# Latent attention with a ternary feed-forward layer on one core: queries and keys stored as scaled 16-bit high and low parts

## The chip, the core and the metric

The kernel runs on one core of a Trainium2 chip. A core has five engines that run their own instruction streams and meet at semaphores: TensorE (PE; its weight loads are listed as PEld), VectorE (DVE), ScalarE (ACT), GpSimd (POOL) and SyncE (SP), which here only issues transfers. Operands lie in SBUF (128 partitions), matmul results in PSUM. The metric is the device time of one launch in microseconds (us), lower is better.

## What is computed

Two sequences (B = 2) of S = 1024 tokens with D = 256 features go through latent attention with H = 16 heads, a layer norm, a feed-forward layer with ternary weights and a second layer norm:

```python
c_kv = x @ w_dkv;  c_q = x @ w_dq                      # ranks 64 and 192
k_r = rope((x @ w_kr)); q_r = rope(c_q @ w_qr)         # 64 rotary features a head
k_n = c_kv @ w_uk;      q_n = c_q @ w_uq               # 128 plain features a head
scores = einsum('bqhd,bkhd->bhqk', [q_r,q_n], [k_r,k_n]) / sqrt(192)
out = einsum('bhqk,bkhd->bqhd', softmax(scores), c_kv @ w_uv) @ w_o
x = layernorm(x + out)
h1 = x @ t(w1).T; h3 = x @ t(w3).T                     # t(w): ternary weights, HID = 682
y = layernorm(x + (silu(h1) * h3) @ t(w2).T)
```

The attention weights are drawn eight times as large as usual, so the scores are large and their products are made to more than 16 bits: every large operand is kept as a high part and a low part, and a product is made of three terms (high by high, high by low, low by high).

## The kernel before

**Shape of the work.** The products w_uq by w_uk and w_uv by w_o of a head are formed once at the start, so that a head's keys are the 64 latent rows of c_kv under the 64 rotary rows: one key matrix K of 128 rows by 1024 columns serves all heads, and a head's query is a matrix of 128 rows by 1024 columns. The launch has a setup and then a loop over the two batches b, each of which has three stages: the projections (55 to 106 us of the span in the first batch, 518 to 568 in the second), the attention (to 438 and 900) and the output with the feed-forward layer.

**The projections.** `query_terms(g, j, ks)` makes one tile of the queries, ten matmuls of 512 columns (five terms, two column halves), for group g = 0 to 3 of four heads. The tiles j = 0 and 1 are the even and odd rotary rows of four heads, written to the PSUM banks Sa and Sb; the tiles j = 2 and 3 hold the latent rows of two heads each, in Ta/Tb and Oa/Ob. Each pair of banks is used again by the next group, so PE waits until it has been read. DVE multiplies Sa and Sb with the tables of cosines and sines into `qmul` (four products a group, L769, counted by `rope_mul`); POOL adds and subtracts these into `turned` (L361, `rope_sum`), and SP moves `turned` by eight transfers into QO, the queries in fp32. ACT copies the latent rows from Ta/Tb and Oa/Ob into QO (`lat_out`). `turn_values()` transposes the scaled latents of the keys into Oa (eight small matmuls, L1037); ACT and DVE read V_hi and V_lo from it. Before this DVE makes the rotary keys (L724 to L729) into Kf, their largest value and the scale of the values (L741 to L754), and K_lo from K_hi (L757).

**The attention.** A pair p of heads has 16 tiles n of 128 queries, in two half pairs of eight. For a tile: `scores` (six matmuls of 512 columns, L1054) fills Sa or Sb in turn, for the tile two ahead; `maximum` on DVE (a reduction L774, and one operation on a column L777); `exponent` on ACT (L552); `part_high` on ACT (L451) and `low_probs` on POOL (L385) make the 16-bit parts `P_parts` of columns 256 to 1023, which SP transposes by a transfer (L310, `part_in`); columns 0 to 255 are transposed on PE (L1065) and split by ACT (`PT_hi`, L451) and DVE (`PT_lo`, L784). `values` (L1083) sums over the keys for the half pair before, twelve matmuls after every second tile. There are `DEEP` = 4 buffers of probabilities and parts: `part_high` of tile n waits until the transposing transfer of tile n - 4 has landed, and `exponent` of tile n until `low_probs` of tile n - 4 is done. Where a half pair begins, DVE also normalises the sums of the half pair before last (L797, L799) and inverts the sums of the exponentials (L791), ahead of the next `maximum`.

The queries of a pair are split for the scores while the pair before runs: POOL copies four pieces of QO of 512 columns into Q_hi (fp32r, L353) and subtracts them into Q_lo (L347); for the first pair of a batch ACT makes the high parts.

**The output.** `project_out` (L1183) multiplies O_parts with Wvo_hi and Wvo_lo. Wvo_lo was saved to memory at the start, and its place is taken by K_hi and K_lo; ACT issues the transfer back (L605) after the last scores. SP issues xr (the input rows for the residual) and TT (the ternary weights) after the last transposing transfer, and then, in the first batch, Wq_hi and Wq_lo, since their places were overlaid with buffers of the attention.

Everything is written by hand: the order on an engine is the order of the code, and each engine takes its instructions strictly in that order. All transfers that SP issues go through one hardware queue.

## Time and profile before

| | us |
|---|---|
| median of three runs | 986.65 (984.76 to 988.56) |
| time of the profiled execution | 981.67 |
| its span, first to last instruction | 980.0 |
| PE busy | 918.8 (94%) |
| ACT / POOL / DVE busy | 680.4 / 672.0 / 633.7 |
| one pair of heads, 252.26 to 293.99 | 41.73 |

The profile tells for each engine when an instruction began and how long it was busy, and what ended the idle time before it. Busy PE time is a model: matmuls overlap, so the distance between the starts of two matmuls tells more than their length. The mean granted clock of TensorE was 0.989 of full speed. The chain of waits, followed back from the end of the program, runs 56% over PE, 10% over ACT, 9% over DVE, 5% over POOL and 2% over transfers.

### The profile page before, as it was taken

The numbers are of one execution on the slowest core, as the hardware profiler recorded it, in microseconds if no ns is written. First come the engines' busy times: TensorE is split into PE (matmuls) and PEld (weight loads), VectorE is DVE, ScalarE is ACT, GpSimd is POOL, SyncE is SP. The second block draws the span as 40 slices with busy tenths as digits, with TensorE's granted clock in tenths as the row PEclk, the third lists the DMA queues.
The fourth block names the chain that finished last, engine by engine and source line by source line (L and its number), as shares of the span: only waits on it lengthen the run. The fifth ranks groups of instructions, "written<-read, shape, count | busy, mean of one in ns | idle before, by whom it ended". The sixth has DMA issues, their size and how long they took to land.

```text
span 980.0 us, 17588 instructions
## 1 busy us (share of the span) xinstructions
PE 918.8 (94%) x5110; PEld 637.5 (65%) x5110; DVE 633.7 (65%) x1008; ACT 680.4 (69%) x1140; POOL 672.0 (69%) x503
## 2 busy tenths in 40 slices
PE   6799899999999999979989989999999999998985
PEld 3558666666666666658776866666666666666874
DVE  1665677777776677744457667777777777773455
ACT  3735988888878888851334598888878888875132
POOL 0007788988888989760341778889898988875034
PEclk9999999999999999999999999999999999999998
DMA  9834798888787887999000579888787787889201
GB/s 254 260 156 113 141 167 156 147 152 152 150 155 144 152 152 145 160 177 346 16 25 23 129 140 165 149 156 158 144 159 148 147 152 150 151 155 194 118 1 43
DMA packets 419814, 142.24 MB, mean 145 GB/s; under 512 B 405596, under 2 KB 413616, under 8 KB 418736
## 3 DMA queue, kind: packets, MB, share of 16 engines
q1 hardware_dynamic: 418160, 131.11, 67.8%
q10 hardware_dynamic: 1024, 8.39, 2.2%
q0 software_dynamic: 576, 2.10, 0.6%
q8 instruction: 25, 0.41, 0.2%
q14 instruction: 29, 0.24, 0.1%
HBM read 24.38 MB, written 8.13 MB: 33 GB/s over the span
## 4 chain that ended last, share of the span: by engine, by line
PE 56%; issue 15%; ACT 10%; DVE 9%; POOL 5%; DMA 2%; ACTq 1%; DVEq 1%; POOLq 0%
PE Sa L1054 14%; PE Sb L1054 12%; PE Oa L1083 9%; DVE nmax L774 5%; ACT P_parts L451 3%; POOL P_parts L385 3%; ACT probs_a L552 3%; PE Sb L1107 2%; PE Tb L1065 2%; PE Sa L1107 2%; DMA Wvo_lo<-wvo_low 2%; POOL g_lo L427 2%; PE Ta L1065 1%; PE Ob L1093 1%; ACT PT_hi L451 1%
## 5 line engine op out<-in xcount | busy, mean ns | idle before, releaser
L385 POOL TENSOR_TENSOR P_parts<-probs_a,P_parts 128x768 f16<-128x768 f32 x128 | 211.5, 1652 | 43.3 <-ACT P_parts L451 42.1
L385 POOL TENSOR_TENSOR P_parts<-probs_b,P_parts 128x768 f16<-128x768 f32 x128 | 211.6, 1655 | 36.8 <-ACT P_parts L451 36.6
L774 DVE TENSOR_REDUCE nmax<-Sb 128x1 f32<-128x1024 f32 x128 | 156.8, 1225 | 58.2 <-PE Sb L1054 58.2
L774 DVE TENSOR_REDUCE nmax<-Sa 128x1 f32<-128x1024 f32 x128 | 154.8, 1210 | 37.8 <-PE Sa L1054 37.7
L1083 PE MATMUL Oa<-PT_dma,V_hi 128*64 128x512 f16 x768 | 132.3, 385 | 0.0
L552 ACT ACTIVATE probs_b<-Sa,nmax 128x1024 f32<-128x1024 f32 x64 | 71.3, 1114 | 68.4 <-DVE nmax L777 68.2
L361 POOL TENSOR_TENSOR turned<-qmul 128x1024 f32<-128x1024 f32 x16 | 38.1, 2402 | 104.0 <-DVE qmul L769 104.0
L451 ACT ACTIVATE P_parts<-probs_a 128x768 f16<-128x768 f32 x128 | 107.8, 842 | 0.4 <-DMA PT_dma<-P_parts 0.4
L451 ACT ACTIVATE P_parts<-probs_b 128x768 f16<-128x768 f32 x128 | 107.3, 840 | 0.0
L1054 PE MATMUL Sa<-K_hi,Q_hi 128*128 128x512 f32 x256 | 93.1, 445 | 10.0 <-ACT probs_b L552 9.3
L1054 PE MATMUL Sb<-K_hi,Q_hi 128*128 128x512 f32 x256 | 93.5, 446 | 7.2 <-ACT probs_a L552 4.5
L552 ACT ACTIVATE probs_a<-Sa,nmax 128x1024 f32<-128x1024 f32 x64 | 71.4, 1115 | 30.9 <-DVE nmax L777 30.8
L347 POOL TENSOR_TENSOR Q_lo<-QO,Q_hi 128x512 fp32r<-128x512 f32 x64 | 82.2, 1288 | 10.5 <-POOL Q_hi L353 10.5
L1054 PE MATMUL Sa<-K_lo,Q_hi 128*128 128x512 f32 x256 | 80.3, 395 | 0.0
L1054 PE MATMUL Sb<-K_lo,Q_hi 128*128 128x512 f32 x256 | 80.2, 394 | 0.0
L1054 PE MATMUL Sb<-K_hi,Q_lo 128*128 128x512 f32 x256 | 80.0, 394 | 0.0
L1054 PE MATMUL Sa<-K_hi,Q_lo 128*128 128x512 f32 x256 | 79.6, 392 | 0.0
L784 DVE TENSOR_TENSOR PT_lo<-Ta,PT_hi 128x512 f16<-128x512 f32 x64 | 44.3, 692 | 54.6 <-ACT PT_hi L451 54.4
L1054 PEld LDWEIGHTS Sa<-K_hi,Q_hi 128*128 128x128 f32 x256 | 38.4, 188 | 61.8 <-issue 35.4
L1083 PE MATMUL Oa<-PT_dma,V_lo 128*64 128x512 f16 x384 | 73.4, 379 | 0.0
L1083 PEld LDWEIGHTS Oa<-PT_dma,V_hi 128*64 128x64 f16 x768 | 43.2, 109 | 45.2 <-issue 14.0
L552 ACT ACTIVATE probs_a<-Sb,nmax 128x1024 f32<-128x1024 f32 x64 | 71.8, 1121 | 0.1
(293 smaller groups left out, 1946.0 us busy)
## 6 DMA issues: line engine op xcount, KB each, us to landing
QO<-turned SPq DMA_DIRECT2D x64, 128.0 KB, 2.4
TT<-ternary SPq DMA_DIRECT2D x2, 2304.0 KB, 10.8
PT_dma<-P_parts SPq DMA_TRANSPOSE x256, 3.7
ternary<-tern ACTq DMA_DIRECT2D x1, 2304.0 KB, 8.2
wo<-in_L_attn_w_o_dram SPq DMA_DIRECT2D x4, 512.0 KB, 8.5
xq<-in_L_attn_x_dram SPq DMA_DIRECT2D x2, 1024.0 KB, 10.0
wq_high<-Wq_hi ACTq DMA_DIRECT2D x1, 2048.0 KB, 12.8
Wvo_lo<-wvo_low ACTq DMA_DIRECT2D x2, 1024.0 KB, 8.4
```

The source lines that it names most:

```text
L347: nc.gpsimd.tensor_tensor(Q_lo[:, i % 2, cols], QO[:, tile, cols], Q_hi[:, i % 2, cols].bitcast(F), ALU.subtract).then_inc(q_split_lo, 1)
L361: nc.gpsimd.tensor_tensor(turned[:, j, :], qmul[:, 2 * j, :], qmul[:, 2 * j + 1, :], op).then_inc(rope_sum, 1)
L385: nc.gpsimd.tensor_tensor(P_parts[:, n % DEEP, 1, :], probs[n % DEEP][:, KP * P:S], P_parts[:, n % DEEP, 0, :], ALU.subtract).then_inc(par ...
L427: nc.gpsimd.tensor_tensor(g_lo[:, t, :], gate[:, t % 2, :], g_hi[:, t, :].bitcast(F), ALU.subtract).then_inc(glo_done, 1)
L451: return nc.scalar.activation(o, i, ACT.Copy, scale=scale)
L552: nc.scalar.activation(probs[n % DEEP], SS[n % 2][:, :], ACT.Exp, bias=nmax[:, n % 4:n % 4 + 1], accum_out=den[:, n // 8 % 2, n // 4 % 2, ...
L774: nc.vector.tensor_reduce(nmax[:, n % 4:n % 4 + 1], SS[n % 2][:, :], AX.X, ALU.max, negate=True).then_inc(row_max, 1)
L784: nc.vector.tensor_tensor(PT_lo[place].rearrange("p k (t q) -> p t k q", t=2), TS[n // 2 % 2][:, :].rearrange("p (t k q) -> p t k q", t=2, ...
L1054: last = mm(bank[:, m * HALF:(m + 1) * HALF], w[:, a, q:q + P], c[:, m * HALF:(m + 1) * HALF], start=(k == 0), stop=(k == 2))
L1065: last = nc.tensor.transpose(TS[n // 2 % 2][:, at:at + P], probs[n % DEEP][:, k * P:(k + 1) * P], ident[:, :])
L1083: last = mm(Oa[64 * a:64 * a + 64, :], v[:, k, :], pt[:, a, :], start=(k == 0 and i == 0), stop=(k == KT - 1 and i == 2))
L1107: last = mm(Q_BANKS[j][n], w, c[:, n * HALF:(n + 1) * HALF], start=(k == 0), stop=(k == 4))
```

## The change

It stores queries and keys as 16-bit (fp16) high and low parts, each scaled by a power of two.

- **Scales.** At the start DVE takes the largest absolute weight of Wq_hi for each row (two reductions, 128x4096 elements). In each batch DVE takes the largest value of Kf, cq_hi and cq_s for each row (three reductions in the place of one), multiplies and adds columns, PE sums them over the partitions (a matmul of two columns against a matrix of ones), and DVE turns the sums into powers of two: `k_up`, `q_up` and their product's inverse `score_down`.
- **Projections.** Queries go from PSUM into `Q_parts[P, H, 2, S]` (fp16): for latent rows ACT writes the high part with the scale (`latents_high`, one instruction of 128x512 for each bank where there were two of 64x512) and DVE the low part (`latents_low`); SP moves the rows of every second head to its place (eight more transfers a batch). For rotary rows DVE's four products take `q_up`, POOL makes `turned` as before, ACT its 16-bit high part (`rotary_parts_high`, 128x1024), POOL the low part (128x1024), and SP moves both at once, behind the move of the latents. K_hi and K_lo are fp16.
- **Order in the projections.** `turn_values()` moves from tile (0, 2) to just ahead of tile (1, 3) (g, j), and V_lo on DVE from ahead of the first products to behind the products and the first latents of group 1. K_lo comes after the first latents of group 0. The last `latents_low` stands between the first two `maximum`.
- **Attention.** The scores read `Q_parts`, K_hi and K_lo in fp16. The split of the queries is gone from POOL and ACT. `maximum` and `exponent` take `score_down` as a per-partition operand.
- **Memory.** Wvo_lo and xr share the place of Wq_lo; both are fetched by SP when a batch's queries are done, ahead of its first transposing transfer. Wq_hi stays in SBUF; Wq_lo is saved whole and fetched whole after the attention's output, in the first batch.

The core of the diff:

```diff
@@ SP, in the loop over batches
                 for g in range(GROUPS):
+                    for i in range(2):
+                        t = 4 * g + 2 * i
+                        sp.wait_ge(lat_lo, b * 4 * GROUPS + 4 * g + 2 * i + 2)
+                        sp.dma_start(Q_parts[64:128, t, :, :], Q_parts[0:64, t + 1, :, :]).then_inc(lat_moved, 16)
+                    sp.wait_ge(lat_moved, (b * 2 * GROUPS + 2 * g + 2) * 16)
                     for j in range(2):
-                        sp.wait_ge(rope_sum, b * 2 * GROUPS + 2 * g + j + 1)
+                        sp.wait_ge(rope_lo, b * 2 * GROUPS + 2 * g + j + 1)
...
+                for j in range(2):
+                    sp.wait_ge(turned_out[j], (b + 1) * 64 * GROUPS)
+                sp.wait_ge(q_ps, (b + 1) * 4 * GROUPS)
+                sp.dma_start(Wvo_lo[:, :, :].rearrange("p j d -> p (j d)").bitcast(F), wvo_low).then_inc(wvo_in, 16)
+                sp.dma_start(xr[:, :, :], x_v[b]).then_inc(xr_in, 16)
...
-                sp.wait_ge(pv_done, b * 2 * PAIRS + PV0 + 2 * PAIRS - 1)
-                sp.dma_start(xr[:, :, :], x_v[b]).then_inc(xr_in, 16)
@@ POOL
-                    if g == 1:
-                        for i in range(4):
-                            split_low(i % 2, b * PAIRS, i)
+                    for j in range(2):
+                        if g >= 1:
+                            pool.wait_ge(turned_out[j], b * 64 * GROUPS + 64 * g)
+                        pool.wait_ge(rope_hi, b * 2 * GROUPS + 2 * g + j + 1)
+                        nc.gpsimd.tensor_tensor(turned_parts[:, j, 1, :], turned[:, j, :], turned_parts[:, j, 0, :],
+                                                ALU.subtract).then_inc(rope_lo, 1)
...
-                            split_high(p * 2 + 2 + i % 2, pair + 1, i, pair * TILES + 4 * i + 4)
-                            split_low(p * 2 + 2 + i % 2, pair + 1, i)
@@ ACT
                     nc.scalar.activation(probs[n % DEEP], SS[n % 2][:, :], ACT.Exp, bias=nmax[:, n % 4:n % 4 + 1],
+                                         scale=score_down,
                                          accum_out=den[:, n // 8 % 2, n // 4 % 2, n % 4:n % 4 + 1]).then_inc(exp_done, 1)
@@ DVE
-                    nc.vector.tensor_scalar(nmax[:, n % 4:n % 4 + 1], nmax[:, n % 4:n % 4 + 1], PROB_UP_LOG, None,
-                                            ALU.add).then_inc(max_ready, 1)
+                    nc.vector.tensor_scalar(nmax[:, n % 4:n % 4 + 1], nmax[:, n % 4:n % 4 + 1], score_down, PROB_UP_LOG,
+                                            ALU.mult, ALU.add).then_inc(max_ready, 1)
@@ PE
-                            last = mm(bank[:, m * HALF:(m + 1) * HALF], w[:, a, q:q + P], c[:, m * HALF:(m + 1) * HALF],
+                            last = mm(bank[:, m * HALF:(m + 1) * HALF], Q_parts[:, p * 2 + a, part, q:q + P], c[:, m * HALF:(m + 1) * HALF],
```

PE around the transposes of the values. Before, they stand in the middle of the third query tile of group 0 (Ta/Tb), and the next tile (Oa/Ob) waits for V_lo, signalled by `cq_lod`:

```order
L1107 MATMUL Tb<-cq_hi,Wq_lo 128x512
L240 REGISTER_ALU
L1037 MATMUL Oa<-ident,kmul 128x64 [waits k_step]
L1037 MATMUL Oa<-ident,kmul 128x64 x7
L1107 MATMUL Ta<-cq_s,Wq_hi 128x512
L1107 MATMUL Tb<-cq_s,Wq_hi 128x512
L1107 MATMUL Ta<-cq_s,Wq_lo 128x512
L1107 MATMUL Tb<-cq_s,Wq_lo 128x512
L1107 MATMUL Oa<-cq_hi,Wq_hi 128x512 [waits cq_lod]
```

Now, in group 1, between its third and its fourth query tile:

```order
L1156 MATMUL Tb<-cq_s,Wq_lo 128x512
L251 REGISTER_ALU [waits lat_lo]
L1089 MATMUL Oa<-ident,kmul 128x64 [waits k_step]
L1089 MATMUL Oa<-ident,kmul 128x64 x7
L1156 MATMUL Oa<-cq_hi,Wq_hi 128x512 [waits cq_lod]
```

The transposes have moved by four query tiles, and the tile of Oa/Ob behind them still waits for V_lo. That V_lo (L817) on DVE, with what stands ahead of it in group 1 (the products L804 and the low parts of the latents L795):

```order
L804 SCALAR_TENSOR_TENSOR qmul<-Sa,limits,tcos 128x1024 [waits rope_sum]
L803 REGISTER_ALU
L804 SCALAR_TENSOR_TENSOR qmul<-Sa,limits,tsin 128x1024 [waits rope_sum]
L801 REGISTER_ALU
L804 SCALAR_TENSOR_TENSOR qmul<-Sb,limits,tsin 128x1024 [waits rope_sum,q_ps]
L804 SCALAR_TENSOR_TENSOR qmul<-Sb,limits,tcos 128x1024 [waits rope_sum]
L795 SCALAR_TENSOR_TENSOR Q_parts<-Ta,limits,Q_parts 128x512 [waits lat_hi]
L795 SCALAR_TENSOR_TENSOR Q_parts<-Tb,limits,Q_parts 128x512 [waits lat_hi]
L817 TENSOR_TENSOR V_lo<-Oa,V_hi 128x512 [waits v_hi]
```

Before, V_lo (L759) stood ahead of all products. SP at the end of the projections now, down to the first transposing transfer of the attention:

```order
L317 DMA Q_parts<-turned_parts 32x2048 [waits rope_lo]
L317 DMA Q_parts<-turned_parts 32x2048 x3
L325 DMA Wvo_lo<-wvo_low 128x2048 [waits wq_out,q_ps,wvo_out,odd_out,even_out]
L326 DMA xr<-in_L_attn_x_dram 128x8x256
L328 UNCONDITIONAL_BRANCH
L328 ISA
L251 ISA [waits pv_done]
L334 DMA_TRANSPOSE PT_dma<-P_parts 128x12x128 [waits part_lo]
```

The two transfers L325 and L326, of 1 MB each, were not there before; they stand now between the last move of the queries and the first transposing transfer.

## Rows read from the trace of the kernel before

**Rows 1.** Busy time of each engine in one pair: us, engines, PEclk, DMA share, GB/s

```profile
252.26:293.99 41.73, 41.07 (x233) 26.86 (x233) 29.97 (x47) 35.01 (x59) 37.15 (x29) 1.00 0.80 151
```

**Rows 2.** Timeline of PE in a pair: start us, us, engine, line, op, out<-in, xcount

```profile
287.48 0.38 PE L1083 MATMUL Oa<-PT_dma,V_lo 128*64 128x512 f16 x2
287.70 0.60 PE L1083 MATMUL Oa<-PT_dma,V_hi 128*64 128x512 f16 x4
...
288.66 0.73 PE L1054 MATMUL Sa<-K_hi,Q_hi 128*128 128x512 f32 x2
289.23 0.62 PE L1054 MATMUL Sa<-K_lo,Q_hi 128*128 128x512 f32 x2
...
290.16 0.38 PE L1065 MATMUL Ta<-ident,probs_a 128*128 128x128 f32 x2
290.42 0.73 PE L1054 MATMUL Sb<-K_hi,Q_hi 128*128 128x512 f32 x2
```

**Rows 3.** Timeline of the same stretch, where a half pair begins

```profile
285.40 1.22 DVE L774 TENSOR_REDUCE nmax<-Sa 128x1 f32<-128x1024 f32 x1 [0.38 <-PE Sa L1054]
...
286.84 1.11 ACT L552 ACTIVATE probs_a<-Sa,nmax 128x1024 f32<-128x1024 f32 x1 [0.72 <-DVE nmax L777]
...
289.16 1.12 ACT L552 ACTIVATE probs_a<-Sb,nmax 128x1024 f32<-128x1024 f32 x1
...
289.30 0.69 DVE L784 TENSOR_TENSOR PT_lo<-Tb,PT_hi 128x512 f16<-128x512 f32 x1 [0.75 <-ACT PT_hi L451]
...
289.91 0.74 DVE L797 SCALAR_TENSOR_TENSOR O_parts<-Oa,vscale,rden_row 128x512 f32 x1
...
291.33 1.18 DVE L774 TENSOR_REDUCE nmax<-Sa 128x1 f32<-128x1024 f32 x1
...
293.99 0.73 PE L1054 MATMUL Sa<-K_hi,Q_hi 128*128 128x512 f32 x2 [0.28 <-ACT probs_b L552]
```

**Rows 4.** Groups of ACT instructions, 440 to 960 us: xcount | busy, mean ns | idle before

```profile
L552 ACT ACTIVATE probs_a<-Sb,nmax 128x1024 f32<-128x1024 f32 x32 | 35.9, 1121 | 0.0
...
L634 ACT ACTIVATE QO<-Oa,ffs 128x512 f32<-128x512 f32 x11 | 7.5, 679 | 23.3 <-PE Ob L1212 23.3
...
L451 ACT ACTIVATE x1T_hi<-Ta 128x512 fp32r<-128x512 f32 x4 | 2.4, 591 | 23.0 <-PE Tb L1196 23.0
```

**Rows 5.** Timeline of DVE, the first product of the queries of batch 0

```profile
70.78 1.21 DVE L769 TENSOR_TENSOR qmul<-Sa,tcos 128x1024 f32<-128x1024 f32 x1
```

**Rows 6.** Chain that ended last, in order of time: first query tile of group 2

```profile
82.65 2.27 PE Sa L1107 x10
```

**Rows 7.** Timeline of POOL in the projections, group 1

```profile
81.67 4.77 POOL L361 TENSOR_TENSOR turned<-qmul 128x1024 f32<-128x1024 f32 x2 [2.57 <-DVE qmul L769]
```

**Rows 8.** Page, costliest groups: POOL's low parts of the probabilities

```profile
L385 POOL TENSOR_TENSOR P_parts<-probs_a,P_parts 128x768 f16<-128x768 f32 x128 | 211.5, 1652 | 43.3 <-ACT P_parts L451 42.1
```

**Rows 9.** Timeline of ACT: exponential of tile 1, high part of tile 4, first pair

```profile
105.06 1.11 ACT L552 ACTIVATE probs_a<-Sb,nmax 128x1024 f32<-128x1024 f32 x1
...
114.96 0.83 ACT L451 ACTIVATE P_parts<-probs_a 128x768 f16<-128x768 f32 x1
```

**Rows 10.** Page, transfers by line: KB each, us from issue to landing

```profile
QO<-turned SPq DMA_DIRECT2D x64, 128.0 KB, 2.4
```

**Rows 11.** Transfers issued after the first batch's attention, the same columns

```profile
TT<-ternary SPq DMA_DIRECT2D x1, 2304.0 KB, 10.9
...
xr<-in_L_attn_x_dram SPq DMA_DIRECT2D x1, 1024.0 KB, 6.2
```

**Rows 12.** Timeline of SP, where it issues xr; TT's issue follows it

```profile
440.97 0.74 SPq L315 DMA_DIRECT2D xr<-in_L_attn_x_dram  x1
```

**Rows 13.** Timeline of PE at the output projection of either batch

```profile
438.72 1.56 PE L1183 MATMUL Sa<-Wvo_lo,O_parts 128*128 128x256 f32 x7 [3.61 <-DMA Wvo_lo<-wvo_low]
...
900.42 1.86 PE L1183 MATMUL Sa<-Wvo_lo,O_parts 128*128 128x256 f32 x7 [2.66 <-DMA Wvo_lo<-wvo_low]
```

**Rows 14.** Timeline of ACT at the end of the setup

```profile
45.95 1.22 ACTq L518 DMA_DIRECT2D wq_high<-Wq_hi  x1
```

More of the change, by code:

```diff
@@ L292, in _ @@
                 if b:
[L293 removed]
+                    sp.wait_ge(wq_in, 16)
                     sp.sem_inc(wq_ready, 1)
@@ L386, in low_probs, with pair_pool @@
                                             P_parts[:, n % DEEP, 0, :], ALU.subtract).then_inc(part_lo, 1)
-                def pair_pool(p, first, last):
+                def pair_pool(p, first):
                     pair = b * PAIRS + p
@@ L1042, in _, with scores @@
                 pe.wait_ge(wq_ready, b + 1)
[L1044 removed]
+                def scores(tile, n, p):
                     a, q = n // 4 % 2, (n // 8 * 4 + n % 4) * P
[L1047 to L1048 removed]
                     pe.wait_ge(exp_done, tile + 1)
                     bank = SS[n % 2]
[L1052 removed]
+                    for k, (part, c) in enumerate(((0, K_hi), (0, K_lo), (1, K_hi))):
                         for m in range(2):
[L1054 removed]
+                            last = mm(bank[:, m * HALF:(m + 1) * HALF], Q_parts[:, p * 2 + a, part, q:q + P], c[:, m * HALF:(m + 1) * HALF],
                                       start=(k == 0), stop=(k == 2))
```

295 lines of the change are left out of this document (166 added, 129 removed).

## The prediction

> **What bounds the kernel now.** I read first the busy time of the engines in one pair of heads, since 14 of the 16 pairs look alike and fill two thirds of the span. Of 41.73 us PE is busy 41.07, POOL 37.15, ACT 35.01, DVE 29.97, and the transfers 80% [rows 1]. PE looks like the bound, so the timeline of PE comes next. A `scores` takes 1.50 us, from 288.66 to 290.16: the first two matmuls 0.57, the other four 0.93, or 0.2325 each. The 16-bit matmuls of `values` go in twos, side by side in the two halves of the array, and two start every 0.22 us (287.48, 287.70; some 0.215 over a run of them) [rows 2]. Two tiles then take 1.50 + 0.26 + 1.50 + 0.28 + 1.42 = 4.96 us.
>
> But twice a pair PE waits, and the timeline of all engines shows for what. The scores in Sa are done at 285.2; then come DVE's maximum (285.40), the exponential (286.84), ACT's two splits, PT_lo (289.30), the two normalisations (289.91 on), the inversion, the next maximum (291.33), its exponential, and only then PE's next scores into Sa at 293.99 [rows 3]. These 8.8 us hold no PE work. Where the exponential ends last, a matmul that is faster brings nothing. A second such loop, for Sb: from the end of the scores in Sa it is 1.64 us to the exponential of Sa, 2.32 more to that of Sb (289.16), 1.12 for it, so the next scores in Sb can't begin before 5.1 us; they begin at 290.42, 5.2 us after [rows 2, 3]. That leaves 0.1 us.
>
> **The attention: gain from the scores, loss from the scale.** Fp16 scores at the pace of `values` save 6 x 0.017 = 0.10 us. The first two matmuls cost 0.105 more than the later ones, which I put down to a weight load that nothing hides; it may vanish or stay. So a `scores` saves 0.10 to 0.2; I take 0.15, and 0 is the lower bound, as no row shows a 16-bit load of 128 columns.
>
> The exponential now takes a scale from SBUF. A silu of 128x512 that does takes 679 ns, a copy of the same size that doesn't 591: 0.09 us. The exponential already reads its bias from there and writes a sum (1121 ns) [rows 4], so its price lies between 0 and 0.09; I take 0.09, since the silu is the nearest row. The Trainium skill ("ScalarE: Activation LUTs", section "What ACT_TABLE_LOAD costs") says that each per-partition operand of an ACTIVATE adds about 93 ns; this rule speaks against the change, would take the upper end, and the sum below stays as it is. On DVE an operation of three operands with such a scalar took 0.74 against 0.69 without [rows 3], so 0.05 for the column operation behind the maximum.
>
> The stretch with the normalisations holds two exponentials and two such column operations: 8.85 (the mean of its two forms) becomes 9.1. The other 12.0 us of a half pair hold five scores. The first is followed by a wait for the exponential of Sb, which eats its gain. The other four bring 0.6, less 0.06 for that later exponential: 11.5. A half pair takes 20.6 where it took 20.9, and gains 0.3 (0.6 if the scale is free, 0.5 at 0.2 per scores, 0.1 at 0.1). There are 15 half pairs a batch with this shape: 30 x 0.3 = **-9.0** (-3 to -20). The first half pair of a batch has no `values`, and ACT bounds it: 8 x 0.09 a batch, **+1.4**.
>
> POOL loses 4 copies and 4 subtractions a pair. It stands in neither loop, so this brings nothing.
>
> **The projections: a wait where there was none.** PE runs through them without a gap, a query tile of ten matmuls in 2.27 us [rows 6]. I follow the new order with these durations. The rotary products began at 70.78 [rows 5]; ahead of them now go two more reductions (1.2 each, as in [rows 3]), a sum on PE and ten column operations (0.15 to 0.2 each), and K_lo, V_lo and a wait of 1.3 go away: about 71.6. Group 0 on DVE: four products (1.2 each) to 76.4, two low parts of latents (0.7 each, as PT_lo in [rows 3]) to 77.8, K_lo to 79.0, two more low parts to 80.4. Group 1: products to 85.2, two low parts to 86.6, V_lo to 87.3. PE meanwhile starts group 1 at 74.0, has made three tiles by 81.0, transposes the values until 81.9, and then waits for V_lo, since its fourth tile overwrites Oa. It waits 5.4 us. Group 2 starts at 89.5 and not at 82.65 [rows 6]: +6.9.
>
> From there PE is the bound again until the last tile. At the end two things more stand in line on DVE and ACT: the last latents' high parts on ACT behind the exponential of tile 0, then their low parts on DVE ahead of the maximum of tile 1. I get tile 0's scores at 105.0, the last tile at 108.9, its low parts at 112.0, the maximum at 113.5, and the exponential of tile 1 at 113.6, where it was 105.06 [rows 9]. That is +8.5 a batch, **+17.0** (+10 to +22).
>
> **The start of the attention: two megabytes ahead of the first transpose.** POOL gets eight subtractions of 128x1024 a batch. One of 128x768 takes 1.65 [rows 8], so 2.2 each, beside 2.4 for each sum [rows 7]. The last two can't start before ACT's last high parts: 112.4 to 116.8. SP then issues four moves (0.6 each, under the 0.74 of [rows 12]), they land 2.4 us after their issue [rows 10], at 121.4, and only then SP issues Wvo_lo and xr, and behind them the first transposing transfer. That the queue works off one transfer after another shows where it is full: xr landed 6.2 us after its issue; TT was issued 0.86 us later and landed 10.9 after its own, 5.5 us behind xr, for 2.3 MB [rows 11, 12]. So Wvo_lo costs some 2.4 us, xr behind it up to 6.2, and the transposing transfer its own 2.1 (80% of 41.73 over 16 [rows 1]): it lands at about 131.5. Who waits is ACT: the high part of tile 4 needs the buffer of tile 0. It was due at 114.96 [rows 9], and with the shift of 8.3 so far at 123.3. It waits 8.2 us, and all of ACT, DVE and PE behind it; the later tiles follow at 2.1 us each, ACT's own pace there. **+16.4** for both batches, +3.6 at the least (without the two transfers ahead it would land at 125.1) and +20 at the most.
>
> **The ends.** PE waited 3.61 and 2.66 us for Wvo_lo at the output projection [rows 13]. It lies in SBUF now, and PE's own work follows: **-6.3**. What is late next is the residual's input, which arrives long before too.
>
> **The start.** The transfer of Wq_hi to memory goes away; ACT spent 1.22 us on its issue [rows 14] just ahead of the copies for which PE waits: **-1.2**. DVE's reduction over all weights (4096 elements, four times 1.2) fits in the 11 us in which it waits for PE there; without this cover it would cost 5.
>
> **Sum.** -9.0 + 1.4 + 17.0 + 16.4 - 6.3 - 1.2 = +18.3 us on a profiled execution of 981.67 that lies 5 under the median: 1000.0 there, **1005** for the median.
>
> **The rivals.**
> 1. The two transfers don't hold up the first transposes, because transfers overlap or ACT comes later than I reckon: 3.6 in the place of 16.4, 992.1. For it: every transposing transfer lands in time in the profile. Against it: the row of xr and TT.
> 2. PE's wait is not there either, because DVE's low parts are quicker or the projections hide them, and only the 0.9 us of the later first product stay: 986.65 + 1.8 + 1.4 - 9.0 - 6.3 - 1.2 = 973.4, **faster**. It decides where V_lo ends on DVE: by 82 nothing waits, at 87 all does. Against it: four products of group 1 alone end no earlier than 85.
> 3. 16-bit scores run much closer together than any row shows. If a `scores` shortened by 0.6 rather than 0.15, the 12.0 us of a half pair would become 9.5, the loop over the exponentials would take some 0.6 back, and 30 half pairs would bring 54 us in the place of 9: 960. The rows of `values` at 0.215 speak against it. The Trainium skill ("TensorE: Matmul & The Clock Gate", section "Back-to-back issue gap") gives some 131 ns for each matmul of 512 columns in a stream, by which the scores would shorten so; this case's 16-bit rows, two in 0.215 side by side in half arrays, don't show it for the whole array.
> 4. The chain ACT, POOL, SP between the groups is longer than my reckoning: each high part waits behind latents that PE makes late, so the last moves land 3 us later a batch and the stores behind them too, and exponentials that wait for POOL add as much: 12 more, 1017.
>
> **How the numbers follow.** The forecast has 0.58, rival 1 0.18, rival 2 0.07, rival 3 0.05, rival 4 0.12. The forecast's own bounds give 993 to 1014. From 984 to 1018 I leave out rivals 2 and 3 and some of rival 4. Half a per cent, 4.9 us, is about what a measurement of this kernel can tell from no change. Slower by more: the forecast, rival 4 and half of rival 1, 0.78. Within: the other half of rival 1 and a bit, 0.10. Faster: 0.12.
>
> **What the profile would show.** A half pair in steady state of 20.6 us; `scores` of 1.35; exponentials of 1.2. In the projections PE idle for 5 us behind the transposes of the values, released by V_lo. At the first tiles of the attention ACT idle for 8 us ahead of the high part of tile 4, released by a transposing transfer. No wait for Wvo_lo. I would be wrong above all if that ACT wait is short, or if a half pair gains a microsecond.

## The result, and the profile after

The changed kernel takes 1022.5 us (median of four runs, 1017.6 to 1024.2), the kernel before 987.6 in the same session: ratio 1.033, 95% interval 1.026 to 1.040. It is slower, as forecast, but by 35 us and not by 18, and the time lies outside my range of 984 to 1018.

The page of the changed kernel: busy time of each engine, and the chain that ended last by engine.

```profile
span 1019.1 us, 17708 instructions
...
PE 891.6 (87%) x5114; PEld 502.5 (49%) x5114; DVE 681.3 (67%) x1060; ACT 695.9 (68%) x1116; POOL 596.0 (58%) x401
...
PE 28%; ACT 25%; issue 20%; DVE 11%; POOL 9%; DMA 3%; ACTq 2%; SPq 1%; POOLq 0%; DVEq 0%
```

PE has 27 us less to do, the chain ran 56% over it before and runs 28% over it now. The work that ends last is spread over PE, ACT and DVE: a sign of a ring of waits, not of one full engine, but no proof of it.

To see where the time went I cut both traces at the same events: DVE's first key product of a batch, the exponential of tile 1, and POOL's sixteen widenings of the reciprocals (`rden_wide`, one for each half pair, so that fifteen half pairs lie between the first and the sixteenth). Both batches are added up.

| us in the profiled execution | before | after | difference | forecast |
|---|---|---|---|---|
| start to the first key product | 55.7 | 57.0 | +1.4 | -1.2 |
| key product to the exponential of tile 1 | 98.8 | 121.7 | +22.8 | +17.0 |
| exponential of tile 1 to the first widening | 42.9 | 64.7 | +21.8 | +17.8 |
| first to sixteenth widening | 618.4 | 623.0 | +4.6 | -9.0 |
| from there to the next key product or the end | 164.2 | 152.7 | -11.6 | -6.3 |
| span | 980.0 | 1019.1 | +39.1 | +18.3 |

**The projections.** Timelines of PE, DVE and ACT after, around the wait for V_lo (start us, us, engine, line, op, count, in brackets idle time and what ended it):

```profile
82.97 0.71 PE L1089 MATMUL Oa<-ident,kmul 64*128 64x64 f32 x8
...
87.96 0.68 DVE L817 TENSOR_TENSOR V_lo<-Oa,V_hi 128x512 f16<-128x512 f32 x1
...
88.70 0.79 PE L1156 MATMUL Oa<-cq_hi,Wq_hi 128*128 128x512 f32 x1 [5.01 <-DVE V_lo L817]
89.29 0.63 PE L1156 MATMUL Ob<-cq_hi,Wq_hi 128*128 128x512 f32 x1
89.72 0.63 PE L1156 MATMUL Oa<-cq_lo,Wq_hi 128*128 128x512 f32 x1
...
117.47 1.21 ACT L566 ACTIVATE probs<-Sb,nmax,limits 128x1024 f32<-128x1024 f32 x1 [0.39 <-DVE nmax L828]
```

The wait is there, with 5.0 us for my 5.4. The exponential of tile 1 begins at 117.47, where it was 105.06 [rows 9]. But behind it two matmuls stand 0.43 us apart, where before and later on it is 0.23.

**The start of the attention.** Timelines of SP, ACT and PE after:

```profile
125.80 0.34 SPq L325 DMA_DIRECT2D Wvo_lo<-wvo_low  x1
126.18 0.44 SPq L326 DMA_DIRECT2D xr<-in_L_attn_x_dram  x1
...
135.93 0.84 ACT L451 ACTIVATE P_parts<-probs 128x768 f16<-128x768 f32 x1 [7.20 <-DMA PT_dma<-P_parts]
...
138.01 1.03 PE L1103 MATMUL Sa<-K_hi,Q_parts 128*128 128x512 f16 x2 [7.54 <-ACT probs L566]
138.84 1.06 PE L1103 MATMUL Sa<-K_lo,Q_parts 128*128 128x512 f16 x2
```

ACT waits 7.2 us here and 9.8 in the second batch, 17.0 against my 16.4. This wait also differs from batch to batch, from 6.8 to 10.6 us in the kernels below that leave the order of these transfers alone. Here too PE's matmuls are slow behind the wait. The windows of the trace after give the clock (us of the window, busy time of PE, PEld, DVE, ACT, POOL, then the granted clock as a share of 2.4 GHz, the DMA share and GB/s):

```profile
88.00:93.00 5.00, 4.30 (x11) 3.39 (x12) 0.64 (x2) 0.00 (x0) 3.70 (x2) 0.52 0.86 187
138.00:142.00 4.00, 3.99 (x11) 1.78 (x12) 1.91 (x2) 3.09 (x5) 2.96 (x3) 0.50 1.13 210
```

0.5 is the lower level, 1.2 GHz. Both windows follow a stretch in which PE did nothing.

**The steady attention.** Timelines of all engines after, the way of one score bank round the engines:

```profile
283.34 0.60 PE L1103 MATMUL Sb<-K_hi,Q_parts 128*128 128x512 f16 x2 [0.42 <-ACT probs L566]
...
284.65 0.38 PE L1114 MATMUL Ta<-ident,probs 128*128 128x128 f32 x2
...
284.85 1.23 DVE L825 TENSOR_REDUCE nmax<-Sb 128x1 f32<-128x1024 f32 x1 [0.63 <-PE Sb L1103]
...
286.11 0.22 DVE L828 TENSOR_SCALAR nmax<-nmax,limits 128x1 f32<-128x1 f32 x1
...
286.66 1.21 ACT L566 ACTIVATE probs<-Sb,nmax,limits 128x1024 f32<-128x1024 f32 x1
...
288.10 0.60 PE L1103 MATMUL Sb<-K_hi,Q_parts 128*128 128x512 f16 x2
...
289.39 1.21 ACT L566 ACTIVATE probs<-Sa,nmax,limits 128x1024 f32<-128x1024 f32 x1 [0.71 <-DVE nmax L828]
```

The scores did get shorter, to 1.31 us (283.34 to 284.65) from 1.50 [rows 2]: six matmuls at 0.218. But PE now waits for the exponential (0.42), ACT for the maximum (0.71), DVE for the scores (0.63), each for the next in the ring. The half pair shows in the distance of POOL's widenings after (253.48, 274.54) and before (251.17, 273.29, 292.89, where two unlike ones make a pair):

```profile
253.48 0.62 POOL L384 TENSOR_SCALAR rden_wide<-rden 128x512 f32<-128x512 f32 x1
274.54 0.62 POOL L384 TENSOR_SCALAR rden_wide<-rden 128x512 f32<-128x512 f32 x1
```

It is 21.07 us, where it was 20.87 and I forecast 20.6.

**The ends.** Timeline of PE before, behind its wait for Wvo_lo, and after, at the same products:

```profile
440.07 2.92 PE L1183 MATMUL Sa<-Wvo_hi,O_parts 128*128 128x256 f32 x14
442.83 0.99 PE L1183 MATMUL Sa<-Wvo_lo,O_parts 128*128 128x256 f32 x7
...
447.33 1.84 PE L1183 MATMUL Sb<-Wvo_hi,O_parts 128*128 128x256 f32 x14
```

```profile
460.66 1.75 PE L1243 MATMUL Sa<-Wvo_hi,O_parts 128*128 128x256 f32 x14
```

The wait of 3.61 us [rows 13] cost the kernel before more than its length: fourteen products took 2.92 us behind it, and take 1.75 now. The window of the trace before shows the clock below its upper level: 0.66 from 438 to 443, against 1.00 on both sides.

```profile
433.00:438.00 5.00, 2.10 (x18) 1.73 (x14) 2.12 (x4) 0.29 (x1) 4.35 (x4) 1.00 1.17 193
438.00:443.00 5.00, 4.28 (x23) 4.29 (x24) 0.00 (x0) 0.00 (x0) 0.00 (x0) 0.66 1.09 230
443.00:450.00 7.00, 7.00 (x61) 7.00 (x61) 2.00 (x6) 0.60 (x1) 0.00 (x0) 1.00 1.03 388
```

From 438.72 to 442.83 PE makes 21 products, 4.11 us; 21 such products from 446.49 to 449.01 take 2.52. That is 1.6 us in the first batch. In the second they take 3.89 us behind the wait of 2.66, 1.4 more than 2.52.

### The profile page after: what moved, and what is told of

It is laid out like the page before. It is cut to its first block, busy times and chain, and to the rows that moved or that the text cites. A ratio compares the mean times of both kernels' runs of the same rounds, so it can differ in the third digit from the quotient of the medians.

```text
span 1019.1 us, 17708 instructions
## 1 busy us (share of the span) xinstructions
PE 891.6 (87%) x5114; PEld 502.5 (49%) x5114; DVE 681.3 (67%) x1060; ACT 695.9 (68%) x1116; POOL 596.0 (58%) x401
## 4 chain that ended last, share of the span: by engine, by line
PE 28%; ACT 25%; issue 20%; DVE 11%; POOL 9%; DMA 3%; ACTq 2%; SPq 1%; POOLq 0%; DVEq 0%
ACT probs L566 11%; ACT P_parts L451 8%; POOL P_parts L398 6%; PE Sb L1103 6%; DVE nmax L825 5%; PE Oa L1132 4%; ACT PT_hi L451 3%; PE Sa L1103 3%; DMA PT_dma<-P_parts 2%; ACT rden_row L451 2%; POOL g_lo L427 1%; DVE qmul L804 1%; PE Sa L1156 1%; PE Sb L1156 1%; DVE Q_parts L795 1%
## 5 line engine op out<-in xcount | busy, mean ns | idle before, releaser
L398 POOL TENSOR_TENSOR P_parts<-probs,P_parts 128x768 f16<-128x768 f32 x256 | 420.8, 1645 | 210.2 <-ACT P_parts L451 210.2
L451 ACT ACTIVATE P_parts<-probs 128x768 f16<-128x768 f32 x256 | 214.3, 838 | 17.0 <-DMA PT_dma<-P_parts 17.0
L566 ACT ACTIVATE probs<-Sa,nmax,limits 128x1024 f32<-128x1024 f32 x128 | 154.0, 1203 | 90.3 <-DVE nmax L828 90.1
L825 DVE TENSOR_REDUCE nmax<-Sb 128x1 f32<-128x1024 f32 x128 | 156.5, 1223 | 55.9 <-PE Sb L1103 55.7
L1103 PE MATMUL Sb<-K_hi,Q_parts 128*128 128x512 f16 x512 | 155.1, 385 | 43.6 <-ACT probs L566 42.8
L1103 PE MATMUL Sa<-K_hi,Q_parts 128*128 128x512 f16 x512 | 156.3, 388 | 34.8 <-ACT probs L566 34.7
L566 ACT ACTIVATE probs<-Sb,nmax,limits 128x1024 f32<-128x1024 f32 x128 | 154.3, 1205 | 1.5 <-DVE nmax L828 1.5
L835 DVE TENSOR_TENSOR PT_lo<-Ta,PT_hi 128x512 f16<-128x512 f32 x64 | 44.3, 692 | 65.8 <-ACT PT_hi L451 65.7
L1103 PE MATMUL Sa<-K_lo,Q_parts 128*128 128x512 f16 x256 | 77.6, 385 | 0.0
L1103 PE MATMUL Sb<-K_lo,Q_parts 128*128 128x512 f16 x256 | 77.1, 383 | 0.0
L835 DVE TENSOR_TENSOR PT_lo<-Tb,PT_hi 128x512 f16<-128x512 f32 x64 | 44.2, 691 | 43.3 <-ACT PT_hi L451 43.3
L828 DVE TENSOR_SCALAR nmax<-nmax,limits 128x1 f32<-128x1 f32 x256 | 54.9, 214 | 9.0
L1114 PE MATMUL Tb<-ident,probs 128*128 128x128 f32 x256 | 49.9, 277 | 2.4 <-ACT probs L566 2.4
```

Source lines behind the costliest of these rows:

```text
L398: nc.gpsimd.tensor_tensor(P_parts[:, n % DEEP, 1, :], probs[n % DEEP][:, KP * P:S], P_parts[:, n % DEEP, 0, :], ALU.subtract).then_inc(par ...
L451: return nc.scalar.activation(o, i, ACT.Copy, scale=scale)
L566: nc.scalar.activation(probs[n % DEEP], SS[n % 2][:, :], ACT.Exp, bias=nmax[:, n % 4:n % 4 + 1], scale=score_down, accum_out=den[:, n // 8 ...
L825: nc.vector.tensor_reduce(nmax[:, n % 4:n % 4 + 1], SS[n % 2][:, :], AX.X, ALU.max, negate=True).then_inc(row_max, 1)
L828: nc.vector.tensor_scalar(nmax[:, n % 4:n % 4 + 1], nmax[:, n % 4:n % 4 + 1], score_down, PROB_UP_LOG, ALU.mult, ALU.add).then_inc(max_rea ...
L835: nc.vector.tensor_tensor(PT_lo[place].rearrange("p k (t q) -> p t k q", t=2), TS[n // 2 % 2][:, :].rearrange("p (t k q) -> p t k q", t=2, ...
```

## The experiments

My theory after the result has three parts: the two operands lengthen a ring that bounds the steady attention; the waits of the projections and of the attention's start are the two that I named; and each costs more than its length, since the clock falls in it. The medians come from all executions, and the ratios compare them with the kernel before in the same session. The other columns come from the one profiled execution of each kernel. "Without start" leaves out the weights' stage ahead of the first key product: it took 55 to 57 us in some executions and 60 to 66 in others of like kernels, with a granted clock between 0.50 and 1.00 from 30 to 40 us, and this moves a run by some 9 us. The columns between are those of the table above. "Exp to widening" holds ACT's wait for the first transposing transfer, so a difference of 2 or 3 us in it shows nothing by itself.

| | median us (ratio to before) | key to exp | exp to widening | first to sixteenth widening | without start |
|---|---|---|---|---|---|
| before | 987.6 | 98.8 | 42.9 | 618.4 | 924.4 |
| after | 1022.5 (1.033) | 121.7 | 64.7 | 623.0 | 962.1 |
| before with operands | 1004.9 (1.019) | 99.6 | 44.2 | 634.7 | 941.6 |
| constant scales | 1003.9 (1.018) | 122.0 | 64.1 | 607.0 | 946.0 |
| exponential alone | one run | 121.5 | 62.0 | 612.4 | 948.2 |
| values early | 1012.3 (1.027) | 111.2 | 63.3 | 623.2 | 949.8 |
| transfers later | 1012.7 (1.026) | 122.7 | 48.2 | 624.4 | 949.0 |
| filled wait for V_lo | 1017.0 (1.031) | 117.3 | 63.6 | 623.2 | 956.7 |
| filled attention, misplaced | one run | 121.8 | 65.8 | 623.2 | 963.4 |
| filled attention | one run | 120.7 | 61.4 | 622.9 | 960.5 |
| order mended | 997.9 (1.010) | 112.9 | 47.9 | 623.1 | 937.9 |
| and constant scales | 983.5 (0.996) | 112.6 | 50.9 | 607.0 | 922.1 |
| and no preparation | 975.2 (0.987) | 107.3 | 48.5 | 608.5 | 915.6 |
| and a column for the keys | 975.5 (0.987) | 106.9 | 49.9 | 608.5 | 916.6 |

### The two operands, taken out of the changed kernel

```diff
-  ... ACT.Exp, bias=nmax[...], scale=score_down, ...
+  ... ACT.Exp, bias=nmax[...], scale=2.0 ** -12, ...
-  tensor_scalar(nmax[...], nmax[...], score_down, PROB_UP_LOG, ALU.mult, ALU.add)
+  tensor_scalar(nmax[...], nmax[...], 2.0 ** -12, PROB_UP_LOG, ALU.mult, ALU.add)
-  tensor_scalar(scale_up, pow_inv, FULL, None, ALU.mult)
+  tensor_scalar(scale_up, pow_inv, 0.0, 64.0, ALU.mult, ALU.add)
```

> The changed kernel, with constant scales: keys and queries are scaled by 64, the exponential has the immediate 2^-12 in place of the column score_down, and so has the column op behind the maximum. All operations of the preparation stay, so only these two operands are taken out. Theory A: the attention is bound by a ring of waits, exponential, scores of the same bank, maximum, column op, next exponential, in which the operands stand (exponential 1.20 against 1.12 us, column op 0.21 against 0.15). Without them the half pair falls from 21.07 to 20.5 us (20.2 to 20.8), 32 of them make 10 to 26 us, and the run takes 996 to 1012 us. Theory B: TensorE or the transposing transfers bound the half pair and the operands are hidden: half pair 20.9 to 21.1, run 1018 to 1026 us.

The half pair fell to 20.52 us, and from the first to the sixteenth widening both batches took 16.0 us less. The half pair in POOL's timeline of this run:

```profile
281.73 0.62 POOL L384 TENSOR_SCALAR rden_wide<-rden 128x512 f32<-128x512 f32 x1
302.25 0.62 POOL L384 TENSOR_SCALAR rden_wide<-rden 128x512 f32<-128x512 f32 x1
```

The groups of instructions of this run, 210 to 420 us (count, busy us, mean ns, idle before):

```profile
L566 ACT ACTIVATE probs<-Sa,nmax 128x1024 f32<-128x1024 f32 x42 | 46.8, 1114 | 31.5 <-DVE nmax L828 31.5
...
L828 DVE TENSOR_SCALAR nmax<-nmax 128x1 f32<-128x1 f32 x82 | 12.6, 154 | 2.8
```

and of the changed kernel in the same stretch:

```profile
L566 ACT ACTIVATE probs<-Sa,nmax,limits 128x1024 f32<-128x1024 f32 x40 | 48.2, 1204 | 28.6 <-DVE nmax L828 28.6
...
L828 DVE TENSOR_SCALAR nmax<-nmax,limits 128x1 f32<-128x1 f32 x80 | 17.2, 214 | 2.8
```

So the operands cost 0.09 and 0.06 us a tile by themselves, 1.2 us in the eight tiles of a half pair, and 0.55 of these come through to its length. Without them the half pair is 0.35 us shorter than before. That is what fp16 scores and the missing split of the queries bring together; which of the two, no run tells apart. It is little: eight scores are 8 x 0.20 = 1.6 us shorter, and once in each of four rounds of the ring it would be 0.8. Why only 0.35 come through stays open.

### The exponential alone

Here the column op keeps its column, filled with the constant; keys and queries are scaled by 64 as in the run before.

```diff
-  ... ACT.Exp, bias=nmax[...], scale=score_down, ...
+  ... ACT.Exp, bias=nmax[...], scale=2.0 ** -12, ...
-  scalar_tensor_tensor(score_down, pow_of[:, 0:1], 1.0 / (FULL * FULL), pow_of[:, 1:2], ALU.mult, ALU.mult)
+  tensor_scalar(score_down, pow_of[:, 0:1], 0.0, 2.0 ** -12, ALU.mult, ALU.add)
```

> As the run with constant scales, but only the exponential has its immediate; the column op behind the maximum still takes the column score_down, which holds the constant 2^-12. Theory A: each operation counts in the ring by its own length, so the exponential's 0.09 us, which stands twice in the ring's way of two tiles, carries four fifths: half pair 20.6 us (20.5 to 20.75), between 20.52 without both operands and 21.07 with both. Theory B: VectorE's column op carries it, since it runs right ahead of the exponential while the exponential overlaps with TensorE's other work: half pair 20.85 to 21.0.

20.71 us: of the 0.55 the exponential carries 0.36 and the column op 0.19. That is two thirds and not four fifths, but each counts about four times a half pair by its own length (4 x 0.09, 4 x 0.06 = 0.24). The half pair lies in theory A's range, but A's reason, that the exponential counts twice as often as the column op, is not what the two parts show. Theory B falls.

### The two operands, put into the kernel before

```diff
+  nc.gpsimd.memset(unit[:, :], 1.0)
+  ... ACT.Exp, bias=nmax[...], scale=unit[:, 0:1], ...
-  tensor_scalar(nmax[...], nmax[...], PROB_UP_LOG, None, ALU.add)
+  tensor_scalar(nmax[...], nmax[...], unit[:, 0:1], PROB_UP_LOG, ALU.mult, ALU.add)
```

> The kernel before, with nothing of the change but the two operands of the steady attention: the exponential takes its scale from a column of ones, and the column op behind the maximum multiplies by that column before it adds. The exponential should take 1.20 in place of 1.12 us and the column op 0.21 in place of 0.15. Theory A: the ring exponential, scores, maximum, column op, exponential bounds the attention already in the kernel before, or is so near to TensorE's own work that 0.15 us more a tile makes it the bound: half pair 21.2 to 21.6 in place of 20.87, the run is 10 to 20 us longer than before (ratio 1.010 to 1.020). Theory B, on which my forecast stood: TensorE bounds the attention of the kernel before and ScalarE's and VectorE's tenths are hidden: half pair 20.87 to 20.95, ratio 1.000 to 1.003.

Ratio 1.0185 (1.0128 to 1.0242), span 997.9 against 980.0. Two half pairs take 42.88 us in the place of 41.73:

```profile
236.02 0.61 POOL L372 TENSOR_SCALAR rden_wide<-rden 128x512 f32<-128x512 f32 x1
256.28 0.62 POOL L372 TENSOR_SCALAR rden_wide<-rden 128x512 f32<-128x512 f32 x1
278.90 0.62 POOL L372 TENSOR_SCALAR rden_wide<-rden 128x512 f32<-128x512 f32 x1
```

This decides against the base of my forecast. PE was busy for 98% of a pair [rows 1], and yet 0.09 us more on ACT and 0.06 on DVE for each tile made a half pair 0.57 us longer, nearly four times their sum of 0.15. The ring was as long as PE's own work already before.

### V_lo earlier

```diff
@@ ScalarE, group 1
+                    values_high()
                     latents_high(g, 0)
-                    values_high()
@@ VectorE, in the products of group 1, behind the second of four
+                        if g == 1 and j == 1:
+                            tensor_tensor(V_lo, Oa, V_hi, ALU.subtract)
```

> The changed kernel, with the value parts moved forward on two engines: ScalarE makes V_hi ahead of the latents of tile 2 of group 1, and VectorE makes V_lo after two of the four rotary products of group 1 in place of after all four and two low parts. Theory A: TensorE's wait before tile 3 of group 1 (5.0 us) falls to 1.0 to 2.0, and the ten matmuls behind it run at full clock (0.23 in place of 0.43 us each, another 2 us); the exponential of tile 1 comes 4 to 6 us earlier in each batch, the run takes 1010 to 1015 us. Theory B: VectorE is the bound of the whole projection stage, so that what TensorE no longer waits for here it waits for at the next rotary product: the exponential of tile 1 moves by under 1.5 us a batch, the run takes 1019 to 1023 us.

12.3 us less from the first key product on. PE waits 1.57 us (timeline of PE), and the clock holds at 1.00 (window of the trace):

```profile
93.45 0.50 PE L1156 MATMUL Oa<-cq_hi,Wq_hi 128*128 128x512 f32 x1 [1.57 <-DVE V_lo L808]
```

```profile
92.00:97.00 5.00, 3.55 (x16) 2.93 (x16) 4.83 (x6) 2.77 (x6) 5.00 (x3) 1.00 0.45 98
```

### The wait for V_lo filled with matmuls

```diff
                             turn_values()
+                            for k in range(20):
+                                mm(Ob[:, :], Wq_hi[:, 4, 0, :], cq_hi[:, 0:HALF], start=True, stop=True)
                             pe.wait_ge(cq_lod, b * 4 + 4)
```

> The changed kernel, with twenty matmuls of 128x512 into the free bank Ob, whose result nobody reads, in TensorE's wait for V_lo. They take 20 x 0.23 = 4.6 us and end before the wait does (5.0 us). Theory A: the ten slow matmuls behind the wait (0.43 us each in place of 0.23) are slow because the granted clock fell to its lower level while TensorE had nothing to do; with the filling they take 0.23 and everything behind comes 2.0 us earlier in each batch, the run is 3 to 4 us shorter (1017 to 1020). Theory B: they are slow for another reason, ScalarE and the transfers of the same moment, or a cold start of any matmul after a wait: they stay at 0.43 and the run at 1020 to 1024 us.

The matmuls behind the wait take 0.23 us from the second on, the window from 93 to 96 shows clock 1.00, and the exponential of tile 1 comes 1.8 and 2.6 us earlier:

```profile
88.39 4.86 PE L1187 MATMUL Ob<-cq_hi,Wq_hi 128*128 128x512 f32 x20
93.47 0.50 PE L1156 MATMUL Oa<-cq_hi,Wq_hi 128*128 128x512 f32 x1 [0.23 <-DVE V_lo L817]
93.81 0.39 PE L1156 MATMUL Ob<-cq_hi,Wq_hi 128*128 128x512 f32 x1
```

```profile
93.00:96.00 3.00, 2.77 (x13) 2.11 (x12) 0.42 (x1) 0.00 (x0) 3.00 (x2) 1.00 0.92 204
```

The wait ends no earlier, only PE's idle time is gone: 4.4 us of the 22.8 in the projections are the clock's. The Trainium skill ("TensorE: Matmul & The Clock Gate", section "What's actually happening") says that the slow level is the default and that activity releases it; this trace agrees: the granted clock was 0.52 behind the idle wait and 1.00 behind the filled one.

### Wvo_lo and xr later

```diff
+                turn_parts(0)
                 sp.dma_start(Wvo_lo..., wvo_low)
                 sp.dma_start(xr..., x_v[b])
-                with sp.Fori(0, PAIRS) as p:
+                with sp.Fori(1, PAIRS) as p:
+                    turn_parts(p)
```

> The changed kernel, with the loads of Wvo_lo and xr (2 MB) issued after the sixteen transposing transfers of the first pair in place of ahead of the first. Theory A: the first transposing transfer lands 2 to 3 us after its issue in place of 8.8, ScalarE's wait before the high part of tile 4 (7.2 us) falls to under 1.5, TensorE has no idle of 7.5 us and no scores of 2.6 us behind it; in pair 1 the loads hold one transposing transfer up by 6 to 8 us, of which the four buffers of P_parts cover all but 0 to 2. The run takes 1002 to 1010 us. Theory B: the loads only move the wait: ScalarE waits 5 us or more at the beginning of pair 1 instead, and the run takes 1017 to 1023 us.

The start of the attention is 16.5 us shorter, and pair 1 gives 1.4 back. ACT's wait is 2.1 us a batch, where I expected under 1.5:

```profile
138.98 0.84 ACT L454 ACTIVATE P_parts<-probs 128x768 f16<-128x768 f32 x1 [2.10 <-DMA PT_dma<-P_parts]
```

From the first key product on it is 13.1 us less. By the median it is 9.8, and the time of 1012.7 misses the 1002 to 1010 that I expected.

### The wait at the attention's start filled with matmuls

```diff
+                        if first and n == 4:
+                            pe.wait_ge(lat_lo, b * 4 * GROUPS + 4 * GROUPS)
+                            for k in range(32):
+                                mm(Ob[:, :], Wq_hi[:, 4, 0, :], Wq_hi[:, 0:2, :, :]..., start=True, stop=True)
                         if not (last and n >= TILES - 2):
                             scores(t0 + n + 2, ...)
```

> The changed kernel, with 32 matmuls of 128x512 into the free bank Ob, whose result nobody reads, ahead of the scores of tile 6 of each batch's first pair: 32 x 0.22 = 7 us of work in a wait of 7.5 us. The wait itself stays. Theory A: behind the wait the scores of tiles 6 and 7 take 2.6 us each because the granted clock is at its lower level there; with the filling they take 1.3, and the beginning of the attention (from the exponential of tile 1 to the first widening of the reciprocals, 31.6 and 33.1 us) becomes 2.0 to 3.0 us shorter in each batch. Theory B: ScalarE and VectorE have as much to do there, so that TensorE's slow scores cost nothing: under 0.7 us a batch.

That was a miss of mine: PE stood still ahead of the scores of tile 8, not of tile 6. The filling only pushed the scores of tiles 6 and 7 back, PE still stood idle for 4.3 us, and the clock was 0.50 from 148 to 152 us. Placed two tiles later, with `n == 6`:

> The changed kernel, with the 32 matmuls into the free bank Ob two tiles later than in the run before it, ahead of the scores of tile 8 of each batch's first pair, where TensorE stood still for 7.5 us. Theory A: the wait ends when it did, and the scores of tiles 8 and 9 behind it take 1.3 us each in place of 2.6, since the granted clock stays at its upper level; from the exponential of tile 1 to the first widening it is 2.0 to 3.0 us shorter than in the changed kernel (31.6 and 33.1 us). Theory B: TensorE's slow scores are hidden behind ScalarE and VectorE there, under 0.7 us a batch.

```profile
137.66 0.60 PE L1103 MATMUL Sa<-K_hi,Q_parts 128*128 128x512 f16 x2 [0.59 <-ACT probs L566]
138.10 0.59 PE L1103 MATMUL Sa<-K_lo,Q_parts 128*128 128x512 f16 x2
```

The scores take 1.3 us. The window of the trace gives the clock:

```profile
138.00:142.00 4.00, 3.04 (x16) 1.36 (x13) 2.46 (x4) 3.78 (x6) 2.96 (x3) 1.00 1.15 211
```

From the end of ACT's wait to the first widening it is 11.6 us in both batches, against 13.2 and 13.0 after: 1.5 us a batch. Each theory was half right. Two scores lose 2.6 us to the clock, ACT and DVE hide a part.

### The order mended, then constants, then no preparation

The first of four kernels has the edit of the early values, and the loads of Wvo_lo and xr go in pieces, one behind each transposing transfer of pair 1:

```diff
+                        if spread and n % 2 == 0:
+                            sp.dma_start(Wvo_lo[:, n // 2, :], wvo_low[:, ...]).then_inc(wvo_in, 16)
+                        elif spread:
+                            sp.dma_start(xr[:, n // 2, :], x_v[b][:, n // 2, :]).then_inc(xr_in, 16)
```

> The changed kernel with its measured scales and both operands, and with its order mended at two places: the value parts earlier on ScalarE and VectorE, as in the run with early values, and the loads of Wvo_lo and xr in sixteen pieces of 128 KB, one behind each transposing transfer of the second pair. If the two gains add up (12.3 and 13.1 us by the traces, both counted from the first key product) the execution from the first key product to the end takes 936 to 940 us in place of 962, 12 to 16 more than the kernel before (924.4). If the pieces hold up the transposing transfers, pair 1 is longer than 42.2 us by more than 1. The run takes 993 to 1003 us by the length that the weights' stage has.

937.9 us: the two gains add up but for 1.2 us (24.2 of 25.4), and nothing holds up pair 1. The second kernel has the constants of the first experiment besides:

> As the run with the mended order, and with constant scales, so that neither the exponential nor the column op behind the maximum takes an operand. Theory A, the three gains add up: 15.2 us less than the run with the mended order alone, 921 to 925 us from the first key product to the end, level with the kernel before (924.4): ratio 0.995 to 1.008. Theory B: with the waits gone another engine is late, and the sum is 5 us or more short of that.

922.1 us, 15.8 less: these gains add up too. Ratio 0.996 (0.992 to 0.999). The third leaves the measuring of the scales out:

```diff
-  tensor_reduce(most, Wq_hi..., AX.X, ALU.max, apply_absolute_value=True)
-  tensor_reduce(w_most, most..., AX.X, ALU.max)
-  tensor_reduce(q_most[:, 0:1], cq_hi..., ALU.max, ...)
-  tensor_reduce(q_most[:, 1:2], cq_s..., ALU.max, ...)
...
-  mm(Ob[:, 0:2], ones_b[:, :], limits[:, 0:2], start=True, stop=True)
...
-  scaled(K_hi[:, :], Kf[:, :], k_up)
+  scaled(K_hi[:, :], Kf[:, :], 64.0)
```

> As the run with constant scales, and without the operations that measured the scales: the maximum over the query weights in the weights' stage (two reductions), two reductions of 1.2 us over the compressed queries, nine column ops and a small matmul in each batch. Keys and queries are scaled by the constant 64. The first query product on VectorE comes 16.3 us behind the first key product in the changed kernel; without the operations 12 to 13, and the exponential of tile 1 moves by 2 to 4 us in each batch. Theory A: 913 to 920 us from the first key product to the end, ratio 0.985 to 0.998, faster than the kernel before. Theory B: the chain on ScalarE, GpSimd and SyncE between the groups takes the gain back: under 1 us a batch, ratio 0.995 to 1.008.

915.6 us; ratio 0.987 (0.984 to 0.991). This kernel is 1.3% faster than the one before. It stands on constants chosen for these inputs, where the changed kernel measures its scales for any. The fourth changes one operand of it:

```diff
-  scalar_tensor_tensor(K_lo[:, :], Kf[:, :], 64.0, K_hi[:, :], ALU.mult, ALU.subtract)
+  scalar_tensor_tensor(K_lo[:, :], Kf[:, :], k_up, K_hi[:, :], ALU.mult, ALU.subtract)
```

> As the run without preparation, with one operand changed: VectorE's low part of the keys, K_lo = Kf times 64 minus K_hi, takes the 64 from a column in SBUF and not as an immediate. In the run without preparation this instruction took 3.12 us, beside sums of 128x1024 on GpSimd, and in the changed kernel, with a column, 1.28. Theory A: with the immediate VectorE cannot read SBUF while GpSimd's instruction does, and waits for its end; with the column both go on side by side: K_lo takes 1.3 us, GpSimd's pair of sums 5.5 to 6 in place of 4.8, and the exponential of tile 1 comes 0 to 2 us earlier in each batch. Theory B: the place in the order alone makes it long, and the column changes nothing: 3.1 us. The run takes 971 to 977 us, ratio 0.983 to 0.991, either way.

Theory A falls: with a column, too, K_lo takes 3.12 us. See the last section.

## Why the prediction was right or wrong

**What bounds the kernel** was read wrong, and this is the step that failed. I found both loops and wrote that the second left 0.1 us, but then reckoned the 12.0 us of a half pair outside the normalisations as PE's, and charged the operands only 0.31 us a half pair. The run with operands in the kernel before shows the ring in the whole half pair: 0.57 us came of them, four rounds of 0.15, not 0.31. The second step that failed is a term put at nothing: what the lower clock costs behind a wait.

**Attention, term -9.0, measured +4.6** for the thirty half pairs. The scores became 0.20 shorter, more than my 0.15; the operands' own prices, 0.09 and 0.06 for my 0.09 and 0.05, were right. The Trainium skill ("ScalarE: Activation LUTs", section "What ACT_TABLE_LOAD costs") says that each per-partition operand of an ACTIVATE adds about 93 ns; the exponential's 1204 against 1114 ns agrees. Wrong is what came through: of the scores 0.35 us a half pair (with POOL's relief), where I had 0.6, and of the operands 0.55, where I had 0.31. These 14 us are two thirds of the miss in the trace.

**Projections, +17.0, measured +22.8.** Mechanism, place and wait (5.0 for 5.4 us) were right. What was missing is the lower clock behind the wait, 4.4 us by the filled wait; some 1.4 stay unexplained.

**Start of the attention, +16.4 and +1.4, measured +21.8.** ACT's wait of 17.0 us for 16.4 was right, and the run with later transfers took 16.5 away. The clock adds some 3 us. That run is still 5.3 us slower there than the kernel before; what of this is the operands' (+1.3 in the kernel before with operands) and what the later landing of the first transposes was not tried apart.

**Ends, -6.3, measured -11.6.** The sign was right, and again the clock is missing: with the waits went the slow products behind them, by an estimate from the rows above 1.6 and 1.4 us. Some 0.9 more come from the products' pace, 21 in 2.38 us after the change (460.66 to 463.04) against 2.52. The last 1.4 stay unexplained.

**Start, -1.2, measured +1.4.** Nothing of it shows. Since this stage moves by 9 us from one execution to the next, neither number says much.

**Rivals.** None came. Rival 1 falls by ACT's waits of 7.2 and 9.8 us, rival 2 by the end of V_lo at 88.6 us (87.3 without the later start), past its 87; its sum had moreover left out the start of the attention, of which rival 1 keeps 3.6 us. Rival 3, scores 0.6 shorter through a pace of some 131 ns, falls: a matmul follows the other after 0.218 us, at a clock of 1.00. Rival 4 had nearly the total, 1017. The last moves of the queries did end 4.4 us later than reckoned (L325 is issued at 125.80, for 121.4), but the whole kernel was late by then, by 1.4 us of the start and some 2 of the clock, and ACT's waits are 17.0 us together for my 16.4.

**The range.** It was too narrow for its own terms: all of them at their upper bounds give about 1020 us, not 1014. The measured 1022.5 lies beyond that too.

**In sum** the trace's 39.1 minus 18.3 is 20.8 us: 13.6 the ring, 5.8 and 4.0 the two starts, 2.6 the setup, -5.3 the ends.

## What to carry to other kernels

A pipeline in which one engine is busy for 98% can still be bound by a ring through all engines: follow one buffer round, add up, and if the slack is a tenth of a microsecond, charge in full whatever the ring gets longer in each round (here 0.57 of 4 x 0.15 us came through), and do not count in full what one engine alone gains (here 0.35 of 1.6 us). Measuring this before the change takes one run: put the new cost alone into the old kernel. A wait on TensorE can cost more than its length: behind those of 5.0 and 7.5 us here the matmuls ran at half the clock. Matmuls without use in the wait show how much.
